# 8x8 window attention: rotated keys moved by a TensorE product and two masked ScalarE copies instead of eight DMA transfers

## The chip, the cores and the metric

The kernel runs on one core of a Trainium2 chip. The metric is device time in microseconds (us) of one execution of the whole program; lower is better. TensorE (PE in the profile; PEld are its weight loads), VectorE (DVE), ScalarE (ACT), GpSimd (POOL) and SyncE (SP, which here only issues transfers) run their own instruction streams and meet at semaphores.

## What is computed

An image of shape (4, 64, 64, 64) goes through five blocks: window attention over 8x8 windows, neighbourhood attention, a routed feed-forward block, retention and a binarised layer of experts. The change touches the first block alone:

```python
B, H, W, C = x.shape                 # 4, 64, 64, 64
hd = C // NH                         # 8 heads of 8
N = WH * WW                          # 64 tokens of an 8x8 window
xw = x.reshape(B, H // WH, WH, W // WW, WW, C).transpose(0, 1, 3, 2, 4, 5).reshape(-1, N, C)
qkv = xw @ qkv_w.T + qkv_b
qkv = qkv.reshape(-1, N, 3, NH, hd).transpose(2, 0, 3, 1, 4)
q, k, v = (qkv[0], qkv[1], qkv[2])
q = _rope2(q.reshape(-1, WH, WW, hd)).reshape(-1, NH, N, hd)
k = _rope2(k.reshape(-1, WH, WW, hd)).reshape(-1, NH, N, hd)
attn = jax.nn.softmax(q * hd ** (-0.5) @ jnp.swapaxes(k, -2, -1), axis=-1)
out = (attn @ v).transpose(0, 2, 1, 3).reshape(-1, N, C)
...
return out @ proj_w.T + proj_b
```

`_rope2` rotates pairs of channels of queries and keys by angles that depend on row and column in the window. The whole is `h = tok(x)`, then `h = h + block(layernorm(h))` four times.

## The kernel before

The five blocks run one after the other. The first, here "the 8x8 stage", takes 32 tiles of 512 tokens (8 windows). Its functions are named `tok_...`; each engine has a list of them per tile, and that written order is the order of execution: nothing reorders it. `pairs` unrolls two tiles (`par` 0 and 1) and loops over pairs, with the first and last pair written out. `T1[...]` are the stage's semaphores; `times(n)` is a count.

For tile i the work is, in the order of the data:

- SP `x_in` loads 512 tokens into `xin`. PE `tok_turn` transposes them into bank T (L503), ACT `tok_turned` copies them to `xT` (L869).
- PE `tok_qk` makes queries and keys in one product of 128x128 by 128x512 into bank T (L525) and the pairs' partners in a second of the same size into bank J1 (L526). Of 128 rows, each group of 32 has 8 for queries of a head, 8 for queries of another, then the keys of the same two.
- DVE `tok_rope` multiplies both by cosines and sines and adds them into `rot` (L1051, L1052, L1056).
- Queries and keys of a head stand in different partitions of `rot`, and a product contracts over equal partitions. So SP `k_in` moves the keys: for each of 4 groups of 32 rows and each of 2 heads one transfer of 8 rows by 512 (16 KB) from `rot` to `k_tok` (a view of `tile_a`), eight per tile (L322). The rows of `k_tok` that belong to no key of the head stay zero from a fill at the start.
- PE `tok_max` makes scores in bf16 to find the largest (L545), DVE `tok_max` reduces them (four reductions, L1077), PE `tok_top` transposes the maxima (L554), ACT copies them (L886), PE `tok_scores` makes scores minus maxima in 128 small products (L567 and L572), ACT takes four exponentials (L890).
- PE `tok_v` makes the values in bank T (L533), ACT `tok_v` copies them to `v_tok` in four copies (L879).
- PE `tok_values` makes the sums of the exponentials in bank OT, columns 0 to 255 (L583), and the weighted values in bank AV, columns 0 to 255 (L589). DVE `tok_normalize` takes the reciprocal (L1066) and multiplies into `aT1` (L1069).
- PE `tok_project` projects into bank OT, columns 256 to 511 (L600), DVE `tok_rows` adds the bias into `h` (L1061).

Tiles overlap. While PE works on the scores of tile i, DVE works ahead: its list for tile i is rows(i-1), max(i+1), normalize(i), rope(i+2). PE's is top(i), scores(i), project(i-1), v(i+1), values(i), turn(i+2), max(i+1), qk(i+2). ACT's is top(i), four exponentials (i), v(i+1), turned(i+2). SP's is x_in(i+3), k_in(i+2). The waits that matter for the change:

```python
def tok_max(i, par):                                   # PE
    pe.wait_ge(T1["k_in"], times((i + 1) * 128))
def tok_values(i, par):                                # PE
    pe.wait_ge(T1["exp_done"], times(i * 4 + 4))
    pe.wait_ge(T1["attn_out"], times(i))
    pe.wait_ge(T1["h_done"], times(i))                 # rows(i-1) has read bank OT
def k_in(i, par):                                      # SP
    sp.wait_ge(T1["rope"], times(i + 1))
```

Of the kernel before, what the change touches and what calls it, by code (L numbers as in the profile page):

```python
# [15 lines left out]
P = 128  # L16
# [28 lines left out]
def shape_tables():  # L45
# [14 lines left out]
    t["sin"] = (sin * scale).astype(np.float32)  # L60
    t["top_rows"] = np.broadcast_to((np.arange(P) % 32)[:, None, None] == np.arange(8)[None, :, None], (P, 8, C)).astype(np.float32)
# [36 lines left out]
def build(nc, a, out):  # L98
    ctx = ExitStack()
    with ctx:  # L100
# [21 lines left out]
        w_p1_rows, b_v1, bias1 = sb("w_p1_rows", [P, 2, C]), sb("b_v1", [P, P]), sb("bias1", [P, C])  # L122
        top_rows, ones_32 = sb("top_rows", [P, 8, C]), sb("ones_32", [P, 2, 32])
# [81 lines left out]
        T1 = named("tok", "x_in", "xT_ps", "xT_sb", "qk_ps", "rope_mul", "rope", "k_in", "v_ps", "v_sb", "max_ps", "max_done", "top_ps", "top_sb",  # L205
# [88 lines left out]
        def _(sp):  # L294
# [4 lines left out]
                     (w_p1[:, :], a["w_p1"]), (w_p1_rows[:, :, :], a["w_p1_rows"]), (b_v1[:, :], a["b_v1"]), (top_rows[:, :, :], a["top_rows"]),  # L299
# [17 lines left out]
            def k_in(i, par):  # L317
                sp.wait_ge(T1["rope"], times(i + 1))
                sp.wait_ge(T1["scores"], times((i - 1) * 2))
                for j in range(4):  # L320
                    for e in range(2):
                        sp.dma_start(k_tok[par][32 * j + HD * e:32 * j + HD * (e + 1), e, :],  # L322
                                     rot[32 * j + HD * (e + 2):32 * j + HD * (e + 3), par, :]).then_inc(T1["k_in"], 16)

            def tok(j, par):
                i = j * 2 + par
                if not isinstance(i, int) or i + 3 < NT:
                    x_in(i + 3)
                if not isinstance(i, int) or i + 2 < NT:
                    k_in(i + 2, par)  # L330

            sp.wait_ge(s_const, NCONST)
            x_in(0)
            x_in(1)
            k_in(0, 0)
            x_in(2)
            k_in(1, 1)
            pairs(sp, tok, 2)
# [94 lines left out]
        def _(gp):  # L433
# [3 lines left out]
                     (kpad[:, :, :], 0.0), (tile_a[:, :, :], 0.0), (tile_b[:, :, :], 0.0), (qk3[:, :], 0.0), (qd3[:, :], 0.0), (state[:, :, :], 0.0),  # L437
# [61 lines left out]
        def _(pe):  # L499
# [36 lines left out]
            def tok_max(i, par):  # L536
                pe.wait_ge(T1["k_in"], times((i + 1) * 128))
                for g in range(2):
                    pe.wait_ge(T1["exp_done"], times((i - 1) * 4 + 2 * g + 2))
                    settle(pe)  # L540
                    for p in range(4):
                        for ab in range(2):
                            for j in (2 * g, 2 * g + 1):
                                r = slice(32 * j, 32 * (j + 1))
                                mm = pe.matmul(s_tok[j][C * ab:C * (ab + 1), p * 128:(p + 1) * 128].rearrange("q (s k) -> q s k", s=2),  # L545
                                               top_half(rot[r, par, window(ab, p)]),
                                               k_tok[par][r, :, window(ab, p)].bitcast(BF16).rearrange("r s (k e) -> r s k e", e=2)[:, :, :, 1],
                                               start=True, stop=True)
                    mm.then_inc(T1["max_ps"], 1)
# [25 lines left out]
            def tok_values(i, par):  # L575
# [17 lines left out]
            def tok_project(i):  # L593
                pe.wait_ge(T1["attn_out"], times(i + 1))
                settle(pe)
                for y in range(4):
                    for y2 in range(2):
                        for ab in range(2):
                            at = 32 * (2 * y2 + ab)
                            mm = pe.matmul(bank["OT"][at:at + 32, 256 + y * C:256 + (y + 1) * C], aT1[:, 32 * (2 * y + y2):32 * (2 * y + y2 + 1)],  # L600
# [3 lines left out]
            def tok(j, par):  # L604
# [17 lines left out]
            tok_qk(0)  # L622
            tok_v(0)
# [238 lines left out]
        def _(act):  # L862
# [8 lines left out]

            def tok_v(i, par):
# [9 lines left out]
            def tok(j, par):  # L882
# [8 lines left out]
                if not last or i + 1 < NT:  # L891
                    tok_v(i + 1, 1 - par)
# [3 lines left out]
            tok_turned(0)  # L896
            tok_v(0, 0)
# [85 lines left out]
        def _(dve):  # L983
# [64 lines left out]
            def tok_rope(i, par):  # L1048
# [6 lines left out]
                dve.wait_ge(T1["k_in"], times((i - 1) * 128))  # L1055
                dve.tensor_tensor(rot[:, par, :], t_cos[:, :], t_sin[:, :], ALU.add).then_inc(T1["rope"], 1)  # L1056

            def tok_rows(i):
                dve.wait_ge(T1["proj"], times(i + 1))
                settle(dve)  # L1060
                dve.tensor_tensor(rows(i * 4, 4), bank["OT"][:, 256:512].rearrange("p (t c) -> p t c", t=4),  # L1061
                                  bias1[:, :].rearrange("p (a c) -> p a c", a=1).broadcast_to((P, 4, C)), ALU.add).then_inc(T1["h_done"], 1)

            def tok_normalize(i):
                dve.wait_ge(T1["av_done"], times(i + 1))
                dve.reciprocal(rec1[:, :], bank["OT"][:, 0:256]).then_inc(T1["rec_done"], 1)  # L1066
# [12 lines left out]
            def tok(j, par):  # L1079
# [151 lines left out]
NLOADS = 38  # L1231
NSTRIP = TOK // 256
NCONST = 28
# [60 lines left out]
```

## Time and profile before

| | us |
|---|---|
| median of 3 runs | 2614.84 |
| lowest, highest | 2593.13, 2616.89 |
| the profiled execution | 2611.62 |
| its span, first to last instruction | 2609.8 |
| PE busy in the span | 1993.9 |
| DVE busy | 1362.4 |
| ACT busy | 1059.0 |
| mean granted TensorE clock | 0.833 |

A busy PE is not PE at its peak, since matmuls overlap. The granted clock is the share of full speed that TensorE had: 1.00 is 2.4 GHz, 0.50 is 1.2 GHz, and there is no other level here. The 8x8 stage lies between about 40 us (first load done) and 551 us of the span. Idle time of an engine is put down to what came last by the profile; of several semaphores it may name the wrong one.

### The profile page before, as it was taken

What the parts mean: (1) busy time and instruction counts of PE and PEld (TensorE: products, weight loads), DVE (VectorE), ACT (ScalarE), POOL (GpSimd) and SP (SyncE); (2) the same over time, 40 slices, a digit from 0 to 9 for tenths busy, and PEclk for the clock granted to TensorE, in tenths of its full rate; (3) what the DMA queues carried; (4) which work ended last, traced back from release to release, by engine and by line L of the source; (5) the groups of instructions that cost most, each with busy time, mean ns of one, the idle gap of its engine ahead of it and who ended that gap; (6) DMA issues with size and microseconds to landing.
All of it is one profiled execution on the core that took longest, in us unless ns stands there. A gap on an engine that the chain in (4) does not pass through costs nothing.

```text
span 2609.8 us, 98500 instructions
## 1 busy us (share of the span) xinstructions
PE 1993.9 (76%) x37794; PEld 1494.9 (57%) x37794; DVE 1362.4 (52%) x3822; ACT 1059.0 (41%) x1826; POOL 451.5 (17%) x416
## 2 busy tenths in 40 slices
PE   2888888866588888888777877777777777777777
PEld 1655666544466666666555555555555555555555
DVE  2444444457444444444355556555566555665555
ACT  0222222223222222222245555555555555555555
POOL 2000000024222332332111111111111111111110
PEclk9777777778799999999878787788877888877888
DMA  2000000024433333333100000000000000000000
GB/s 90 20 19 16 16 17 16 16 62 103 95 91 96 92 93 96 92 92 95 44 9 9 11 9 10 9 9 10 10 10 9 9 9 11 10 9 9 9 11 6
DMA packets 221125, 94.80 MB, mean 36 GB/s; under 512 B 171090, under 2 KB 207762, under 8 KB 220818
## 3 DMA queue, kind: packets, MB, share of 16 engines
q1 hardware_dynamic: 221074, 94.08, 14.8%
q8 instruction: 37, 0.61, 0.1%
q14 instruction: 14, 0.11, 0.0%
HBM read 62.74 MB, written 18.42 MB: 31 GB/s over the span
## 4 chain that ended last, share of the span: by engine, by line
issue 34%; PE 21%; SPq 19%; DVE 12%; POOL 8%; ACT 3%; DVEq 1%; POOLq 0%; DMA 0%; ACTq 0%
SPq L391 10%; PE ps_D L761 4%; POOL rstd_ret L455 3%; ACT prob L945 3%; SPq L380 3%; POOL rstd_bin L455 3%; POOL rstd_ffn L455 2%; DVE prob L1168 2%; PE ps_OT L810 2%; PE ps_AV L771 2%; SPq L362 2%; PE ps_T L822 2%; PE ps_J L827 2%; PE ps_OT L811 1%; PE ps_J L817 1%
## 5 line engine op out<-in xcount | busy, mean ns | idle before, releaser
L945 ACT ACTIVATE prob<-ps_D 128x1024 bf16<-128x1024 f32 x512 | 516.5, 1024 | 254.0 <-PE ps_D L761 253.9
L1168 DVE TENSOR_TENSOR prob<-prob,xb 128x1024 bf16<-128x1024 bf16 x512 | 352.5, 689 | 129.2 <-ACT prob L945 123.3
L761 PE MATMUL ps_D<-g,w_parts 128*128 128x256 bf16 x2048 | 365.4, 309 | 4.3 <-ACT prob L945 0.2
L761 PEld LDWEIGHTS ps_D<-g,w_parts 128*128 128x128 bf16 x2048 | 213.5, 114 | 84.8 <-issue 31.7
L1123 DVE TENSOR_REDUCE m_sb<-ps_D 128x4 f32<-128x400 f32 x256 | 135.3, 570 | 209.7 <-PE ps_D L667 194.1
L933 ACT ACTIVATE prob<-ps_D 100x512 f32<-100x512 f32 x256 | 139.0, 595 | 218.3 <-PE ps_D L689 218.3
L771 PEld LDWEIGHTS ps_AV<-pair_sel,prob 128*128 128x128 bf16 x4096 | 185.0, 101 | 70.8 <-DVE prob L1168 47.1
L455 POOL TENSOR_TENSOR rstd_ffn<-veps_ffn,minus_half 128x2 f32<-128x2 f32 x64 | 59.3, 927 | 890.5 <-DVE veps_ffn L995 890.5
L771 PE MATMUL ps_AV<-pair_sel,prob 128*128 128x2 bf16 x4096 | 182.0, 165 | 40.2 <-DVE prob L1168 39.5
L470 POOL TENSOR_TENSOR tile_a<-q_st,q_mask 128x1024 f32<-128x1024 f32 x64 | 123.4, 1927 | 410.6 <-DMA q_st<-q_d 277.1
L503 PE MATMUL ps_T<-ident,xn_f 128*64 128x128 f32 x128 | 38.8, 407 | 196.8 <-DVE xn_f L1007 191.6
L1077 DVE TENSOR_REDUCE top<-ps_D 128x8 f32<-128x512 f32 x128 | 79.5, 683 | 192.7 <-PE ps_D L545 192.7
L689 PE MATMUL ps_D<-tile_a,key_patch 64*100 64x128 f32 x2048 | 177.4, 288 | 1.0 <-issue 1.0
L685 PE MATMUL ps_D<-mT,key_rows 64*100 64x128 bf16 x1024 | 129.9, 224 | 51.2 <-ACT mT L922 32.2
L689 PEld LDWEIGHTS ps_D<-tile_a,key_patch 64*100 64x100 f32 x2048 | 147.4, 166 | 1.4 <-issue 1.4
L503 PEld LDWEIGHTS ps_T<-ident,xn_f 128*64 128x64 f32 x128 | 11.7, 139 | 212.9 <-issue 212.9
L455 POOL TENSOR_TENSOR rstd_pre<-veps_pre,minus_half 128x4 f32<-128x4 f32 x32 | 32.7, 1022 | 544.1 <-DVE veps_pre L995 544.1
L572 PE MATMUL ps_D<-rot,tile_a 32*64 32x64 f32 x4096 | 124.2, 277 | 3.4 <-issue 3.4
L567 PE MATMUL ps_D<-top_T,top_rows 32*64 32x64 bf16 x2048 | 112.1, 221 | 16.6 <-ACT top_T L886 14.7
L572 PEld LDWEIGHTS ps_D<-rot,tile_a 32*64 32x64 f32 x4096 | 119.0, 175 | 5.8 <-issue 5.8
L685 PEld LDWEIGHTS ps_D<-mT,key_rows 64*100 64x100 bf16 x1024 | 79.9, 123 | 70.3 <-issue 70.3
L503 PE MATMUL ps_T<-ident,xn 128*64 128x128 f32 (+1 forms) x256 | 52.8, 314 | 82.5 <-DVE xn L1007 82.5
(159 smaller groups left out, 3948.9 us busy)
## 6 DMA issues: line engine op xcount, KB each, us to landing
tile_b<-v_d SPq DMA_DIRECT2D x640, 40.0 KB
key_st<-k_d SPq DMA_DIRECT2D x64, 175.0 KB, 3.0
key_st<-k_d SPq DMA_DIRECT2D x64, 167.0 KB, 3.0
w_exp<-experts SPq DMA_DIRECT2D x64, 129.0 KB, 2.2
k_d<-kpad SPq DMA_DIRECT2D x32, 140.0 KB, 2.3
xin<-in_x SPq DMA_DIRECT2D x32, 128.0 KB, 2.1
tile_a<-rot SPq DMA_DIRECT2D x256, 16.0 KB
q_d<-q_sb SPq DMA_DIRECT2D x32, 128.0 KB, 2.4
```

The lines of the kernel that those rows point to most:

```text
L391: sp.dma_start(v_patch[r * KS:(r + 1) * KS, par, :, :], bass.AP(src.tensor, src.offset, [[C, KS], [QP * C, 16], [1, C]])).then_inc(T2["v_i ...
L455: gp.tensor_tensor(rstd[:, :], veps[:, :], minus_half[:, 0:veps.shape[1]], ALU.pow).then_inc(q["rstd"], 1)
L470: gp.tensor_tensor(q_block[:, par, :].rearrange("c (p h q) -> c p h q", h=NH, q=NQ), q_st[:, :].rearrange("c (p a q) -> c p a q", a=1, q=N ...
L572: mm = pe.matmul(s_tok[j][m, at], k_tok[par][r, e, window(ab, p)], rot[r, par, window(ab, p)], start=False, stop=True)
L685: pe.matmul(s_loc[x][0:NKL, u * P:(u + 1) * P], top_half(key_rows[rows_of(x), par, at * NKL:(at + 1) * NKL]), mT[rows_of(x), par, :], star ...
L689: mm = pe.matmul(s_loc[x][0:NKL, u * P:(u + 1) * P], key_patch[rows_of(x), par, at * NKL:(at + 1) * NKL], q_block[rows_of(x), par, at * P: ...
L761: mm = pe.matmul(double[k % 2][:, u * 256:(u + 1) * 256], w_parts[:, (k * 4 + u) * P:(k * 4 + u + 1) * P], g3[:, half, :], start=True, sto ...
L771: mm = pe.matmul(bank["AV"][:, t * C + (k * 4 + u) * 2:t * C + (k * 4 + u) * 2 + 2], prod[:, k % 2, u * 256 + t * P:u * 256 + (t + 1) * P] ...
L933: act.activation(prob1[0:NKL, 2 * g + x, :], s_loc[x][0:NKL, :], ACT.Exp).then_inc(T2["exp_done"], 1)
L945: act.activation(sgn[:, k % 2, :], double[k % 2][:, :], ACT.Sign).then_inc(BN["sign"], 1)
L1123: dve.tensor_reduce(m_sb[:, C * x + HOT[x] + 4 * g:C * x + HOT[x] + 4 * g + 4], m_loc[x][:, 0:4 * NKL].rearrange("p (u n) -> p u n", u=4), ...
L1168: dve.tensor_tensor(prod[:, k % 2, :].rearrange("p (u n) -> p u n", u=4), sgn[:, k % 2, :].rearrange("p (u n) -> p u n", u=4), xb2[:, 1 - ...
```

## The change

Only the 8x8 stage changes, in four ways.

1. The eight transfers of `k_in` and the fill of `tile_a` go. A constant 128x128 matrix `key_shift` has a one where a key row of `rot` is to land in a query row. PE `tok_keys` multiplies `rot` by it into bank J1 (128x128 by 128x512, f32), and ACT `tok_keys` copies the bank twice into `k_tok`, each time scaled by one column of `head_row`, which is 1 in the rows of that head and 0 elsewhere. SP's list is left with `x_in` alone, in a plain loop. Two constants more are loaded.
2. DVE's list becomes rows(i-1), max(i+1), rope(i+2), normalize(i).
3. The sums of the exponentials go to bank AV, columns 256 to 511, beside the values; the projection goes to bank OT, columns 0 to 255. The wait for `h_done` moves from `tok_values` to `tok_project`.
4. PE's list becomes top(i), scores(i), keys(i+1), v(i+1), project(i-1), values(i), turn(i+2), max(i+1), qk(i+2); ACT's becomes top(i), four exponentials, keys(i+1), v(i+1), turned(i+2).

```diff
+    own = (np.arange(P)[:, None] == np.arange(P)[None, :] + 2 * HD) & (use < 2)[None, :]
+    t["key_shift"] = own.astype(np.float32)
+    t["head_row"] = (use[:, None] == np.arange(2)[None, :]).astype(np.float32)
...
-            def k_in(i, par):
-                sp.wait_ge(T1["rope"], times(i + 1))
-                sp.wait_ge(T1["scores"], times((i - 1) * 2))
-                for j in range(4):
-                    for e in range(2):
-                        sp.dma_start(k_tok[par][32 * j + HD * e:32 * j + HD * (e + 1), e, :],
-                                     rot[32 * j + HD * (e + 2):32 * j + HD * (e + 3), par, :]).then_inc(T1["k_in"], 16)
...
             x_in(0)
-            x_in(1)
-            k_in(0, 0)
-            x_in(2)
-            k_in(1, 1)
-            pairs(sp, tok, 2)
+            with sp.Fori(1, NT) as i:
+                x_in(i)
...
             def tok_qk(i):
                 pe.wait_ge(T1["xT_sb"], times(i + 1))
                 pe.wait_ge(T1["rope_mul"], times(i * 2))
+                pe.wait_ge(T1["k_sb"], times(i * 2))
...
+            def tok_keys(i, par):
+                pe.wait_ge(T1["rope"], times(i + 1))
+                settle(pe)
+                pe.matmul(bank["J1"][:, :], key_shift[:, :], rot[:, par, :], start=True, stop=True).then_inc(T1["k_ps"], 1)
...
             def tok_max(i, par):
-                pe.wait_ge(T1["k_in"], times((i + 1) * 128))
+                pe.wait_ge(T1["k_sb"], times((i + 1) * 2))
...
                 pe.wait_ge(T1["attn_out"], times(i))
-                pe.wait_ge(T1["h_done"], times(i))
...
-                        pe.matmul(bank["OT"][32 * j:32 * (j + 1), 0:256], ones_32[:, e, :],
+                        pe.matmul(bank["AV"][32 * j:32 * (j + 1), 256:512], ones_32[:, e, :],
...
             def tok_project(i):
                 pe.wait_ge(T1["attn_out"], times(i + 1))
+                pe.wait_ge(T1["h_done"], times(i))
...
                 tok_scores(i, par)
+                if not last or i + 1 < NT:
+                    tok_keys(i + 1, 1 - par)
+                    tok_v(i + 1)
                 if not last or i:
                     tok_project(i - 1)
-                if not last or i + 1 < NT:
-                    tok_v(i + 1)
                 tok_values(i, par)
...
+            def tok_keys(i, par):
+                act.wait_ge(T1["k_ps"], times(i + 1))
+                for e in range(2):
+                    act.activation(k_tok[par][:, e, :], bank["J1"][:, :], ACT.Copy, scale=head_row[:, e:e + 1]).then_inc(T1["k_sb"], 1)
...
-                tok_normalize(i)
                 if not last or i + 2 < NT:
                     tok_rope(i + 2, par)
+                tok_normalize(i)
```

PE's rows as they stand in the program, from the end of one tile's scores to the next tile's `tok_top` (`tile_a` is the keys, `tile_b` the values, `xT` the tokens). Before:

```order
L572 MATMUL ps_D<-rot,tile_a 64x64 x4
L600 MATMUL ps_OT<-w_p_rows,aT 32x64 x16
L533 MATMUL ps_T<-w_v,xT 64x64 x8
L583 MATMUL ps_OT<-prob,ones 32x256 x8
L589 MATMUL ps_AV<-prob,tile_b 32x64 x32
L503 MATMUL ps_T<-ident,xin 64x128 x4
L545 MATMUL ps_D<-tile_a,rot 64x128 x32
L525 MATMUL ps_T<-xT,w_qk 128x512
L526 MATMUL ps_J<-xT,w_qk_swap 128x512
```

The same place after the change:

```order
L564 MATMUL ps_D<-rot,tile_a 64x64 x4
L518 MATMUL ps_J<-rot,key_shift 128x512
L525 MATMUL ps_T<-w_v,xT 64x64 x8
L592 MATMUL ps_OT<-w_p_rows,aT 32x64 x16
L574 MATMUL ps_AV<-prob,ones 32x256 x8
L580 MATMUL ps_AV<-prob,tile_b 32x64 x32
L489 MATMUL ps_T<-ident,xin 64x128 x4
L537 MATMUL ps_D<-tile_a,rot 64x128 x32
L512 MATMUL ps_T<-xT,w_qk 128x512
L513 MATMUL ps_J<-xT,w_qk_swap 128x512
```

The key product stands between scores and values' weights, the projection has moved behind `tok_v`, and nothing else moved. DVE's rows of one tile, before:

```order
L1061 TENSOR_TENSOR h<-ps_OT,bias 128x256
L1077 TENSOR_REDUCE top<-ps_D 128x8 x4
L1066 RECIPROCAL rec<-ps_OT 128x256
L1069 TENSOR_TENSOR aT<-ps_AV,rec 128x4x8x8
L1051 TENSOR_TENSOR t_cos<-ps_T,cos 128x512
L1052 TENSOR_TENSOR t_sin<-ps_J,sin 128x512
L1056 TENSOR_TENSOR rot<-t_cos,t_sin 128x512
```

DVE's rows of one tile, after:

```order
L1061 TENSOR_TENSOR h<-ps_OT,bias 128x256
L1077 TENSOR_REDUCE top<-ps_D 128x8 x4
L1052 TENSOR_TENSOR t_cos<-ps_T,cos 128x512
L1053 TENSOR_TENSOR t_sin<-ps_J,sin 128x512
L1056 TENSOR_TENSOR rot<-t_cos,t_sin 128x512
L1066 RECIPROCAL rec<-ps_AV 128x256
L1069 TENSOR_TENSOR aT<-ps_AV,rec 128x4x8x8
```

The rotation stands ahead of the reciprocal and the product with it. ACT's rows of one tile after the change, with the two copies of the keys between exponentials and values:

```order
L885 ACTIVATE top_T<-ps_D 128x128
L889 ACTIVATE prob<-ps_D 128x512 x4
L869 ACTIVATE tile_a<-ps_J,head_row 128x512 x2
L878 ACTIVATE tile_b<-ps_T 64x4x4x8 x4
L863 ACTIVATE xT<-ps_T 64x512
```

Before, the same list without the row of L869.

## Rows read from the trace of the kernel before

**Rows 1.** The page: busy time, share of the span and instructions by engine.
```profile
PE 1993.9 (76%) x37794; PEld 1494.9 (57%) x37794; DVE 1362.4 (52%) x3822; ACT 1059.0 (41%) x1826; POOL 451.5 (17%) x416
```

**Rows 2.** Timeline of ACT, L886, once per tile: start, length, idle before.
```profile
60.64 0.28 ACT L886 ACTIVATE top_T<-ps_D 128x128 bf16<-128x128 f32 x1 [9.67 <-PE ps_D L554]
74.75 0.28 ACT L886 ACTIVATE top_T<-ps_D 128x128 bf16<-128x128 f32 x1 [2.81 <-PE ps_D L554]
88.92 0.28 ACT L886 ACTIVATE top_T<-ps_D 128x128 bf16<-128x128 f32 x1 [3.09 <-PE ps_D L554]
...
535.81 0.28 ACT L886 ACTIVATE top_T<-ps_D 128x128 bf16<-128x128 f32 x1 [9.00 <-PE ps_D L554]
```

**Rows 3.** Waits of PE from 137.51 to 506.19 us: total us, times, longest.
```profile
PE ps_D L545 <- DMA tile_a<-rot: 38.4, 12, 3.2
```

**Rows 4.** Windows: length, busy us of PE, PEld, DVE, ACT, POOL, granted clock, DMA.
```profile
137.51:506.19 368.68, 305.94 (x8664) 222.40 (x8664) 165.20 (x241) 93.83 (x240) 0.00 (x0) 0.72 0.09 17
...
302.66:316.32 13.66, 9.67 (x364) 6.98 (x362) 6.88 (x10) 4.50 (x11) 0.00 (x0) 1.00 0.09 19
316.32:333.39 17.07, 15.83 (x360) 11.56 (x361) 6.88 (x10) 3.32 (x9) 0.00 (x0) 0.50 0.08 16
```

**Rows 5.** Windows of an early stretch, the same columns.
```profile
77.38:84.20 6.82, 6.32 (x156) 4.76 (x150) 1.32 (x3) 2.53 (x8) 0.00 (x0) 0.50 0.10 19
```

**Rows 6.** Timeline of PE: start, length, work, idle before.
```profile
302.90 0.55 PE L545 MATMUL ps_D<-tile_a,rot 32*64 32x128 bf16 x32
303.84 1.10 PE L525 MATMUL ps_T<-xT,w_qk 128*128 128x512 f32 x2 [0.39 <-ACT xT L869]
304.78 1.02 PE L526 MATMUL ps_J<-xT,w_qk_swap 128*128 128x512 f32 x2
...
309.56 0.65 PE L600 MATMUL ps_OT<-w_p_rows,aT 128*32 128x64 f32 x32
310.15 0.68 PE L533 MATMUL ps_T<-w_v,xT 64*64 64x64 f32 x16
311.33 1.07 PE L583 MATMUL ps_OT<-prob,ones 128*32 128x256 f32 x16 [0.50 <-ACT tile_b L879]
...
313.30 0.60 PE L503 MATMUL ps_T<-ident,xin 128*64 128x128 f32 x4
317.10 0.81 PE L545 MATMUL ps_D<-tile_a,rot 32*64 32x128 bf16 x32 [3.20 <-DMA tile_a<-rot]
317.84 2.08 PE L525 MATMUL ps_T<-xT,w_qk 128*128 128x512 f32 x2
319.71 1.91 PE L526 MATMUL ps_J<-xT,w_qk_swap 128*128 128x512 f32 x2
...
333.62 0.56 PE L545 MATMUL ps_D<-tile_a,rot 32*64 32x128 bf16 x32
```

**Rows 7.** Timeline of DVE in the same tile as the first rows of group 6.
```profile
305.78 1.75 DVE L1066 RECIPROCAL rec<-ps_OT 128x256 f32<-128x256 f32 x1
...
309.40 0.69 DVE L1056 TENSOR_TENSOR rot<-t_cos,t_sin 128x512 f32<-128x512 f32 x1 [0.22 <-DVE t_sin L1052]
310.65 0.42 DVE L1061 TENSOR_TENSOR h<-ps_OT,bias 128x256 f32 x1 [0.55 <-PE ps_OT L600]
```

**Rows 8.** Timeline of ACT in the same tile.
```profile
309.67 1.09 ACT L890 ACTIVATE prob<-ps_D 128x512 f32<-128x512 f32 x2 [0.17 <-PE ps_D L572]
310.88 0.89 ACT L879 ACTIVATE tile_b<-ps_T 64x128 f32<-64x128 f32 x4
```

**Rows 9.** Timeline of SP: issue of two constants, and of one tile's eight key transfers.
```profile
11.79 1.05 SPq L310 DMA_DIRECT2D key_rows<-in_key_rows  x2
...
310.21 5.32 SPq L322 DMA_DIRECT2D tile_a<-rot  x8
```

**Rows 10.** Timeline of PE, the first tile's `tok_max`.
```profile
56.01 0.81 PE L545 MATMUL ps_D<-tile_a,rot 32*64 32x128 bf16 x32 [5.67 <-DMA tile_a<-rot]
```

**Rows 11.** Timeline of DVE, the last step of the 8x8 stage.
```profile
550.79 0.42 DVE L1061 TENSOR_TENSOR h<-ps_OT,bias 128x256 f32<-128x256 f32 x1 [0.98 <-PE ps_OT L600]
```

More of the change, by code:

```diff
@@ L122, in build @@
         w_p1_rows, b_v1, bias1 = sb("w_p1_rows", [P, 2, C]), sb("b_v1", [P, P]), sb("bias1", [P, C])
+        key_shift, head_row = sb("key_shift", [P, P]), sb("head_row", [P, 2])
         top_rows, ones_32 = sb("top_rows", [P, 8, C]), sb("ones_32", [P, 2, 32])
@@ L203, in settle @@
             eng.sem_inc(s_settled, 1)
-        T1 = named("tok", "x_in", "xT_ps", "xT_sb", "qk_ps", "rope_mul", "rope", "k_in", "v_ps", "v_sb", "max_ps", "max_done", "top_ps", "top_sb",
+        T1 = named("tok", "x_in", "xT_ps", "xT_sb", "qk_ps", "rope_mul", "rope", "k_ps", "k_sb", "v_ps", "v_sb", "max_ps", "max_done", "top_ps", "top_sb",
                    "scores", "exp_done", "av_done", "rec_done", "attn_out", "proj", "h_done")
@@ L298, in _ @@
                      (decay_k[:, :], a["decay_k"]), (w_qk[:, :], a["w_qk"]), (w_qk_swap[:, :], a["w_qk_swap"]), (w_v1[:, :], a["w_v1"]),
-                     (w_p1[:, :], a["w_p1"]), (w_p1_rows[:, :, :], a["w_p1_rows"]), (b_v1[:, :], a["b_v1"]), (top_rows[:, :, :], a["top_rows"]),
+                     (w_p1[:, :], a["w_p1"]), (w_p1_rows[:, :, :], a["w_p1_rows"]), (b_v1[:, :], a["b_v1"]), (top_rows[:, :, :], a["top_rows"]), (key_shift[:, :], a["key_shift"]), (head_row[:, :], a["head_row"]),
                      (w_kq2[:, :], a["w_kq2"]), (w_v2[:, :], a["w_v2"]), (w_p2[:, :, :], a["w_p2"]), (bias2[:, :], a["b_p2"].broadcast_to((P, C))),
@@ L436, in _ @@
                      (ones_row[:, :], 0.0), (ones_row[0:1, :], 1.0), (minus_half[:, :], -0.5), (zeros[:, :], 0.0),
-                     (kpad[:, :, :], 0.0), (tile_a[:, :, :], 0.0), (tile_b[:, :, :], 0.0), (qk3[:, :], 0.0), (qd3[:, :], 0.0), (state[:, :, :], 0.0),
+                     (kpad[:, :, :], 0.0), (tile_b[:, :, :], 0.0), (qk3[:, :], 0.0), (qd3[:, :], 0.0), (state[:, :, :], 0.0),
                      (g3[:, :, :], 0.0), (w_parts[:, :], 0.0), (experts[:, :, NEXP:NEXP + 1, :], 0.0),
@@ L599, in tok_project @@
                             at = 32 * (2 * y2 + ab)
-                            mm = pe.matmul(bank["OT"][at:at + 32, 256 + y * C:256 + (y + 1) * C], aT1[:, 32 * (2 * y + y2):32 * (2 * y + y2 + 1)],
+                            mm = pe.matmul(bank["OT"][at:at + 32, y * C:(y + 1) * C], aT1[:, 32 * (2 * y + y2):32 * (2 * y + y2 + 1)],
                                            w_p1_rows[:, ab, :], start=True, stop=True)
@@ L622, in _ @@
             tok_qk(0)
+            tok_keys(0, 0)
             tok_v(0)
@@ L891, in tok @@
                 if not last or i + 1 < NT:
+                    tok_keys(i + 1, 1 - par)
                     tok_v(i + 1, 1 - par)
@@ L896, in _ @@
             tok_turned(0)
+            tok_keys(0, 0)
             tok_v(0, 0)
@@ L1054, in tok_rope @@
                 dve.wait_ge(T1["scores"], times((i - 1) * 2))
-                dve.wait_ge(T1["k_in"], times((i - 1) * 128))
                 dve.tensor_tensor(rot[:, par, :], t_cos[:, :], t_sin[:, :], ALU.add).then_inc(T1["rope"], 1)
@@ L1060, in tok_rows @@
                 settle(dve)
-                dve.tensor_tensor(rows(i * 4, 4), bank["OT"][:, 256:512].rearrange("p (t c) -> p t c", t=4),
+                dve.tensor_tensor(rows(i * 4, 4), bank["OT"][:, 0:256].rearrange("p (t c) -> p t c", t=4),
                                   bias1[:, :].rearrange("p (a c) -> p a c", a=1).broadcast_to((P, 4, C)), ALU.add).then_inc(T1["h_done"], 1)
@@ L1065, in tok_normalize @@
                 dve.wait_ge(T1["av_done"], times(i + 1))
-                dve.reciprocal(rec1[:, :], bank["OT"][:, 0:256]).then_inc(T1["rec_done"], 1)
+                dve.reciprocal(rec1[:, :], bank["AV"][:, 256:512]).then_inc(T1["rec_done"], 1)
                 dve.wait_ge(T1["rec_done"], times(i + 1))
@@ L1228, in _ @@
             staggered(dve, strips)
-NLOADS = 38
+NLOADS = 40
 NSTRIP = TOK // 256
-NCONST = 28
+NCONST = 27
 def _with_bias(w, b):
```

6 lines of the change are left out of this document (removed).

## The prediction

> **What bounds the kernel now.** I read the page first. PE is the busiest engine by far [rows 1], but a share over five blocks says nothing about one of them, so the next view is the one row that ACT writes per tile of the 8x8 stage, L886 [rows 2]. From 60.64 to 535.81 us it comes 32 times, so 31 tiles take 475.2 us, 15.33 us each. The change touches these 475 us, the fill before them and the tail behind them, and nothing of the other 2,060 us.
>
> Inside, PE is busy 305.9 of 368.7 us, at a mean granted clock of 0.72 [rows 4]. Its largest wait is for the eight key transfers: 38.4 us in 12 of 24 tiles, 3.2 us each [rows 3]. Every second tile waits, and the windows show why the others don't. The stage alternates between 13.66 us at clock 1.00 and 17.07 us at 0.50, together two tiles [rows 4]. In the fast stretch PE reaches the key wait at 313.90 and the transfers land at 317.10; the clock is at half from 316.32, just behind this wait [rows 4, 6]. At half speed PE takes so much longer that the next keys are there in time: 333.62 has no wait in its row [rows 6]. So the stage is bound by PE, and the transfers cost twice: once as 3.2 us of waiting, once by what follows, 17 us at half clock.
>
> The chain behind the wait: DVE's `rot` ends at 310.09 [rows 7], SP issues eight transfers in 5.32 us from 310.21 [rows 9], and 317.10 is 7.0 us behind `rot`.
>
> **The change part by part.** First the price of a tile in which PE waits for no keys.
>
> At full clock, from 302.90 (`tok_max`) to the end of `tok_turn` at 313.30 + 0.60 = 313.90 is 11.00 us [rows 6]. Of this 0.50 us is the wait ahead of the sums at 311.33. The row names ACT, which is not plausible for a copy that starts at 310.88; DVE's `h` ends at 310.65 + 0.42 = 311.07 and `tok_values` waits for it because sums and projection share bank OT [rows 6 to 8]. The sums move to bank AV, so I take the 0.50 off. The new product is 128x128 by 128x512 in f32, as L525 is, which takes 304.78 - 303.84 = 0.94 us. New tile at full clock: 11.00 - 0.50 + 0.94 = 11.44 us.
>
> At half clock, from 317.10 to 333.62 is 16.52 us without a wait for keys or `h` [rows 6]. The product is 319.71 - 317.84 = 1.87 us. New tile at half clock: 18.39 us.
>
> Do the new steps wait for anybody? I put them into the fast tile of group 6, where slack is least.
> - `tok_keys(i+1)` needs `rot` of the next tile. Before, the rotation stood behind the reciprocal (1.75 us from 305.78) and its product (about 0.42, as the bias add of that size takes), and ended at 310.09, 0.5 us after the scores gave way at 309.56 [rows 6, 7]. Now it goes ahead of these 2.2 us and ends near 308. It is hidden by the scores, with 1.5 us to spare. Without the third part of the change PE would wait 0.7 us here.
> - What is late instead is `aT1`, now at about 310.3, for the projection. That one has moved behind key product and `tok_v`: 309.56 + 0.94 + 0.68 = 311.2. Slack 0.9 us.
> - ACT finishes the exponentials at 309.67 + 1.09 = 310.76, then two copies of 128x512. No row shows this form. The nearest is the exponential of the same size, two in 1.09 us [rows 8], and I take that: 310.76 to 311.95 with the start behind it. The values' four copies (0.89 us) end at 312.85. PE wants the keys at `tok_max`, about 314.3, the bank T free at `tok_turn`, about 313.7. Slack 0.8 us. From below the copies could cost half of it, from above twice (2.2 us); then `tok_turn` would wait 0.3 us, 9 us over the stage.
> - SP loses all but one transfer per tile; nobody is queued behind it. `xin` is still asked for when `tok_turn` has read it and has a whole tile to land.
>
> The Trainium skill has something against this way of copying: ScalarE: Activation LUTs, section "What ACT_TABLE_LOAD costs", adds about 93 ns for a scale that is a column in memory. No row here shows such a copy. By it the two take 1.3 us, the slack shrinks by 0.2 us to 0.6, and the sum stays.
>
> Now the clock, which decides more than all of this. If a tile spends the share s of its time at half clock, PE does 1/11.44 of a tile per us at full and 1/18.39 at half, so it lasts 11.44 / (1 - 0.378 s). Before, s was 17.07 of 30.73, 0.56. The trigger in the steady part, the wait for keys, is gone. It isn't the only trigger, however: at 77.38 the clock fell for 6.8 us although PE had waited for no transfer, while it did the small products of the scores, which leave most of the array idle [rows 5]. That tile took 88.92 - 74.75 = 14.17 us [rows 2]. In the steady fast stretches, one of which is in group 4, the scores ran through without a fall. I take the middle between a fall in no tile (s = 0) and one in each (6.8 of 14.2, s = 0.48), a fall in every second tile: s = 0.25, 12.63 us per tile.
>
> The skill's page TensorE: Matmul & The Clock Gate, section "Why this matters for your kernels", asks for no idle gaps between bursts of matmuls and promises the full clock for it. The fall at 316.32 behind the wait agrees with it, the one at 77.38 does not. By the page alone s would be 0 and the time 2486; by the rows it is 2524.
>
> The sum, against the profiled execution of 2611.6:
> - 31 tiles x (15.33 - 12.63) = 83.7 us less.
> - Start: two more loads, as issued two constants take 1.05 us [rows 9]. The first `tok_max` stands at 56.01 behind a wait of 5.67 us for keys [rows 10], so its `rot` was there 7.0 us earlier, at 49.0. The new path from there is key product (1.87), two copies (1.2), the values' copies behind them (0.9) and `tok_turn` (0.6 at full clock, 1.0 taken), 54.0. Together 2.0 - 1.05, 1.0 us less.
> - Tail: from 535.81 to 551.21 [rows 2, 11] are 15.4 us, the same work at about the same mix; at 12.63/15.33 of it, 2.7 us less.
> - Together 87.4: 2524.2 us. The profiled execution is 3 us under the median of the three runs, which themselves spread by 24 us.
>
> **The rivals.**
> - *The clock never falls* (s = 0). For it: scores at full clock ran through in the steady stretches. 31 x 3.89 = 120.6, tail 3.9, start 1.0: 2486 us.
> - *It falls as often as before* (s = 0.48 to 0.56), because the cause is the mixture of small products and not the wait. Tiles of 13.98 to 14.48 us save 42 to 26 us, with tail and start 2567 to 2584.
> - *It falls in each tile and the extra product is paid in full*: the early tile of 14.17 us had no key wait already. With 0.94 to 1.87 us on top it is 15.1 to 16.0, against 15.33. Then the time is 2604 to 2632, no change. Against it: that tile stood in the first pass through the code and contains stalls of issue of its own.
> - *Slower*: the stage locks at half clock. The price is 31 x 3.06 = 95 us, 2709 with the tail; it decides from s = 0.67, where the new tile reaches 15.33. For it: PE was busy 15.83 of 17.07 us and the clock still stayed at half [rows 4], and the change takes idle time away, not small products. Against it: each such stretch of the trace ended at the sums and values, and the new order puts key product, `tok_v`, projection, sums and values in one unbroken piece: at full clock 0.94 + (313.30 - 309.56 - 0.50) = 4.2 us, at half 1.87 + 3.24 x 16.52 / 10.50 = 7.0 us [rows 6].
> - *ScalarE becomes late*: 9 us more by the bound above, 2533, inside the first case.
>
> **How the numbers follow.** Between s = 0.1 and 0.45 (2500 to 2562): 0.50. No falls to speak of: 0.17. As often as before: 0.14. In each tile at full price: 0.12. Slower: 0.07. The time is that of the first, 2524. The range 2484 to 2586 takes in the first three. About 1% is what a measurement of this kernel can tell from no change, 26 us; the first three lie beyond it, so faster 0.81, same 0.12, slower 0.07.
>
> **What the profile after would show.** L886 once in 11.4 to 14 us, 12.6 in the mean. No wait for `tile_a` ahead of the bf16 scores, and none ahead of the sums. Windows of half clock that begin inside the scores and fill a quarter of the stage. The key product at 0.94 and 1.87 us, behind the scores without a wait; two ACT copies in 1.1 to 1.3 us that end before `tok_turn`. I would be wrong if the granted clock of the stage stayed at 0.72 or below, if PE waited for ACT at `tok_turn` or for `aT1` at the projection, or if a tile at full clock took over 12 us.

## The result, and the profile after

| | before | after |
|---|---|---|
| median, us | 2613.26 (4 runs) | 2510.65 (4 runs) |
| lowest, highest | 2593.13, 2616.89 | 2504.36, 2517.65 |
| the profiled execution | 2611.62 | 2515.59 |
| its span | 2609.8 | 2513.8 |
| mean granted clock | 0.833 | 0.871 |

The ratio is 0.962, 95% interval 0.957 to 0.967. The change is faster by 3.8%; 2524 was forecast. One run of the kernel before, measured beside runs 9 to 12, took 8405.6 us and is in none of the ratios.

The page's first part for the kernel after, as in [rows 1]:

```profile
PE 1930.8 (77%) x37858; PEld 1442.6 (57%) x37858; DVE 1363.8 (54%) x3822; ACT 1093.4 (43%) x1890; POOL 464.0 (18%) x415
```

64 matmul records more (two per product), ACT 34 us more, DVE the same. ACT's row once per tile, as in [rows 2]:

```profile
60.02 0.28 ACT L885 ACTIVATE top_T<-ps_D 128x128 bf16<-128x128 f32 x1 [3.87 <-PE ps_D L546]
...
105.61 0.28 ACT L885 ACTIVATE top_T<-ps_D 128x128 bf16<-128x128 f32 x1 [2.75 <-PE ps_D L546]
122.48 0.28 ACT L885 ACTIVATE top_T<-ps_D 128x128 bf16<-128x128 f32 x1 [2.74 <-PE ps_D L546]
133.76 0.28 ACT L885 ACTIVATE top_T<-ps_D 128x128 bf16<-128x128 f32 x1 [2.75 <-PE ps_D L546]
...
442.43 0.28 ACT L885 ACTIVATE top_T<-ps_D 128x128 bf16<-128x128 f32 x1 [4.49 <-PE ps_D L546]
```

31 tiles take 382.4 us, 12.34 us each, where it was 15.33. Twenty of them last 11.28 to 11.31 us, as from 122.48 to 133.76; these run at clock 1.00 throughout and are called full tiles below. They look like this on PE (timeline of the kernel after, to be laid beside [rows 6]):

```profile
215.59 0.55 PE L537 MATMUL ps_D<-tile_a,rot 32*64 32x128 bf16 x32
216.44 1.10 PE L512 MATMUL ps_T<-xT,w_qk 128*128 128x512 f32 x2 [0.29 <-ACT xT L863]
217.37 1.02 PE L513 MATMUL ps_J<-xT,w_qk_swap 128*128 128x512 f32 x2
218.70 0.30 PE L546 MATMUL ps_D<-ident,top 128*128 128x128 f32 x1 [0.31 <-DVE top L1077]
...
222.25 1.12 PE L518 MATMUL ps_J<-rot,key_shift 128*128 128x512 f32 x2
223.31 0.68 PE L525 MATMUL ps_T<-w_v,xT 64*64 64x64 f32 x16
223.92 0.65 PE L592 MATMUL ps_OT<-w_p_rows,aT 128*32 128x64 f32 x32
224.39 1.07 PE L574 MATMUL ps_AV<-prob,ones 128*32 128x256 f32 x16
...
226.88 0.55 PE L537 MATMUL ps_D<-tile_a,rot 32*64 32x128 bf16 x32
...
233.53 2.00 PE L518 MATMUL ps_J<-rot,key_shift 128*128 128x512 f32 x2
```

No row waits for keys, for `h` or for the rotation. What PE mainly waits for still is in its waits from 123 to 442 us, as in [rows 3]:

```profile
PE ps_D L559 <- ACT top_T L885: 12.4, 27, 0.5
PE ps_D L546 <- DVE top L1077: 9.5, 27, 1.5
PE ps_T L512 <- ACT xT L863: 7.6, 26, 0.3
```

The clock, as in [rows 4]: the first four tiles, the other 27, and one fall of the clock, with the stretch of its tile ahead of it.

```profile
60.02:122.48 62.46, 50.89 (x1420) 33.82 (x1420) 25.55 (x38) 20.22 (x49) 0.00 (x0) 0.81 0.05 12
122.48:442.43 319.95, 289.43 (x9793) 200.95 (x9793) 186.84 (x271) 135.32 (x324) 0.00 (x0) 0.95 0.06 14
226.88:233.60 6.72, 5.66 (x231) 4.02 (x230) 6.09 (x8) 1.96 (x4) 0.00 (x0) 1.00 0.09 20
233.60:237.02 3.42, 3.42 (x39) 1.80 (x42) 0.42 (x1) 2.54 (x6) 0.00 (x0) 0.51 0.00 0
```

From 0.73 the clock rises to 0.95 for 27 tiles. It still falls: at 233.60, just behind the scores, although PE had been idle for nothing longer than 0.46 us in this tile. This fall lasts 3.4 us, and its tile 12.82 us instead of 11.28. Of the six falls between the fifth and the thirtieth tile two are of this kind; the other four last 6.8 us each, in tiles of 14.4 us.

### The profile page after: what moved, and what is told of

Same layout as the page of the kernel before. It is cut to its first block, busy times and chain, and to the rows that moved or that the text cites. A ratio compares the mean times of both kernels' runs of the same rounds, so it can differ in the third digit from the quotient of the medians.

```text
span 2513.8 us, 98479 instructions
## 1 busy us (share of the span) xinstructions
PE 1930.8 (77%) x37858; PEld 1442.6 (57%) x37858; DVE 1363.8 (54%) x3822; ACT 1093.4 (43%) x1890; POOL 464.0 (18%) x415
## 3 DMA queue, kind: packets, MB, share of 16 engines
q1 hardware_dynamic: 217266, 89.94, 14.4%
## 4 chain that ended last, share of the span: by engine, by line
issue 32%; PE 27%; SPq 14%; DVE 13%; POOL 8%; ACT 4%; DMA 1%; DVEq 1%; POOLq 0%; ACTq 0%
SPq L377 6%; PE ps_D L755 4%; ACT prob L946 3%; POOL rstd_ffn L441 3%; POOL rstd_ret L441 2%; POOL rstd_bin L441 2%; PE ps_AV L765 2%; DVE prob L1168 2%; PE ps_T L489 2%; SPq L348 2%; PE ps_OT L804 2%; SPq L366 2%; PE ps_T L816 2%; PE ps_J L821 2%; PE ps_J L811 1%
## 5 line engine op out<-in xcount | busy, mean ns | idle before, releaser
L441 POOL TENSOR_TENSOR rstd_ffn<-veps_ffn,minus_half 128x2 f32<-128x2 f32 x64 | 73.7, 1151 | 880.4 <-DVE veps_ffn L996 880.4
L1192 DVE TENSOR_SCALAR g<-ps_J 24x256 bf16<-24x256 f32 x64 | 26.3, 412 | 159.8 <-PE ps_J L811 159.8
L950 ACT ACTIVATE xnT<-ps_T 64x256 f32<-64x256 f32 x64 | 24.2, 378 | 191.3 <-PE ps_T L489 191.3
L923 ACT ACTIVATE mT<-ps_T 128x128 bf16<-128x128 f32 x64 | 17.8, 278 | 204.0 <-PE ps_T L668 204.0
```

The costliest lines, as they stand in the source:

```text
L441: gp.tensor_tensor(rstd[:, :], veps[:, :], minus_half[:, 0:veps.shape[1]], ALU.pow).then_inc(q["rstd"], 1)
```

## The experiments

All times are medians, with the ratio to the kernel before measured beside them. "Tile" is the distance of ACT's rows in the profiled execution; a "fall" is a stretch at 0.50 that begins in the 31 tiles.

**1. The transfers put back, the rest kept.**

```diff
-            with sp.Fori(1, NT) as i:
-                x_in(i)
+            x_in(1)
+            k_in(0, 0)
+            x_in(2)
+            k_in(1, 1)
+            pairs(sp, tok, 2)
...
-                    tok_keys(i + 1, 1 - par)
```

> The changed kernel with the eight key transfers put back in place of the product and the two copies; VectorE's new order, the sums beside the values and PE's new order are kept. Theory (a loop through the transfers): before, tok_max at 302.90 and the keys' arrival at 317.10 are 14.2 us apart; the rotation now stands 2.2 us earlier, so the loop is 12.0 us. PE's own work at full clock is 11.28 - 0.94 = 10.3 us, so PE waits 1.7 us per tile. If such a wait does not pull the clock down, tiles take 12.0 to 13 us and the time is 2510 to 2540. Rival (any wait for keys pulls the clock down): tiles of 14.5 to 15.3 us, 2585 to 2613.

Measured: 2547.3 us, ratio 0.974 (0.969 to 0.980). PE's largest wait from 124 to 466 us, and two rows of its timeline that are one tile apart:

```profile
PE ps_D L549 <- DMA tile_a<-rot: 29.5, 20, 1.9
```
```profile
167.25 0.59 PE L549 MATMUL ps_D<-tile_a,rot 32*64 32x128 bf16 x32 [1.67 <-DMA tile_a<-rot]
...
179.35 0.59 PE L549 MATMUL ps_D<-tile_a,rot 32*64 32x128 bf16 x32 [1.54 <-DMA tile_a<-rot]
```

The loop is there: 12.10 us per tile at full clock, 12.0 expected, with 1.67 us of waiting in it. The time is 7 us above the range expected, and the clock falls 19 times and not 10; 29% of the stage is at half. Seven of the 19 begin 1.0 to 1.7 us behind the end of a wait for keys, where the kernel after has none, so such a wait does cost clock, as the rival said, but not in every tile. Still, with the transfers in place the kernel gains 63 us from the other three parts of the change together. That it is the rotation ahead of the normalisation follows from the loop, 2.1 us shorter as computed; this run does not take the parts apart.

**2. The product and the copies alone in the kernel before.**

```diff
                 if not last or i:
                     tok_project(i - 1)
                 if not last or i + 1 < NT:
+                    tok_keys(i + 1, 1 - par)
                     tok_v(i + 1)
```

> The kernel before with the key product and the two masked copies alone: old VectorE order, sums in bank OT behind the wait for h, projection ahead of the product. Theory: at full clock 11.0 us, plus 0.94 for the product, plus 0 to 0.2 of waiting for the rotation, that is 12.0 us, and falls of the clock as in the changed kernel (0.7 to 1.0 us per tile): 12.8 us, 2535. Rival (the order and the bank carry the gain, or the product only makes PE longer): tiles of 14 us and more, 2575 or above.

Measured: 2527.3 us, ratio 0.9665 (0.961 to 0.972). Full tiles last 11.40 us, 0.12 more than after the whole change, and there are 14 falls. So the first part alone brings 83 of 100 us. Runs 1 and 2 gain 63 and 83 us, together far more than the whole: they shorten the same loop at two places. 12.0 us were expected for a full tile, and 12.8 in the mean, which is what it has: the full tiles are shorter and the falls more than expected. PE does the projection while the rotation ends, and the wait for `h` is covered by the product: among the waits of run 2 from 123 to 456 us neither has a row.

**3. The wait for keys filled with dense products, in the kernel before.** The three products write a bank that nobody reads any more.

```diff
             def tok_max(i, par):
+                pe.wait_ge(T1["rope_mul"], times((i + 1) * 2))
+                settle(pe)
+                for _ in range(3):
+                    pe.matmul(bank["J1"][:, :], w_qk[:, :], cos[:, :], start=True, stop=True)
                 pe.wait_ge(T1["k_in"], times((i + 1) * 128))
```

> The kernel before with three products of 128x128 by 128x512 (0.94 us each at full clock) put ahead of tok_max, where PE waits 3.2 us for the keys; their result is not used. Theory (the idle wait is what pulls the clock down): the clock no longer falls behind it, nearly all tiles run at full clock, and the loop through the transfers of 14.2 us sets the pace: 31 x 1.1 us less, 2575 to 2585. Rival (the clock falls through the small products of the scores, whatever PE does in the wait): half the time at half clock with 5.6 us of added work in such a tile, 2613 to 2660.

Measured: 2613.5 us, ratio 1.001 (0.998 to 1.004), the same. Its stage in the window view, and the rows around one filler:

```profile
59.35:531.54 472.19, 409.16 (x11337) 276.89 (x11337) 211.07 (x308) 120.51 (x309) 0.00 (x0) 0.90 0.09 18
```
```profile
166.70 2.74 PE L540 MATMUL ps_J<-cos,w_qk 128*128 128x512 f32 x6
170.05 0.59 PE L549 MATMUL ps_D<-tile_a,rot 32*64 32x128 bf16 x32 [0.60 <-DMA tile_a<-rot]
```

The clock does what the first theory says: 0.90 instead of 0.73, and the falls at the wait are gone. The time does not. Two tiles of three last 14.2 us, the loop through the transfers, as computed; in each third one the clock falls in the scores and it lasts 16.0 us; the first four tiles take 69.5 us where they took 61.3. The time lies at the lower edge of the rival's range, but not for the rival's reason, since 20% of the stage is at half clock and not half of it; the first theory has the loop right and the remaining falls wrong. What follows is more than either said: before the change, a clock that never fell could not have brought the tiles under 14.2 us. The half clock of the kernel before cost 15.33 - 14.2 = 1.1 us per tile, and the loop through VectorE, SP and the transfers cost the rest of the distance to 11.3 us.

**4, 10. The gap behind the transposed maxima filled, in the kernel after.** The product writes a bank that the scores overwrite. Run 10 repeats run 4 with the kernel after (run 9) beside it.

```diff
                 pe.transpose(s_tok[3][:, 0:P], top1[:, :, :].rearrange("q j n -> q (j n)"), ident[:, :]).then_inc(T1["top_ps"], 1)
+                pe.matmul(s_tok[0][:, 0:256], w_qk[:, :], cos[:, 0:256], start=True, stop=True)
```

> The changed kernel with one product of 128x128 by 128x256 (0.47 us at full clock) between tok_top and the scores, where PE is idle for 0.46 us in each tile; its result is overwritten. Theory (the ten falls of the clock in the stage start where small products follow the idle gaps of tok_top): falls vanish outside the first tiles, six of about 2.2 us each, 13 us less: 2495 to 2500. Rival (the falls have to do with the small products alone): as many falls, and the filler costs 0 to 0.5 us per tile: 2510 to 2520.

> The changed kernel with the 128x128 by 128x256 product in the idle 0.46 us behind tok_top, on the same chip as the changed kernel. Theory (the clock falls where the small products of the scores follow an idle gap; filled, it stays): 31 x 0.6 us less than the changed kernel, 2495 to 2503, at most three falls in the stage, all in the first tiles. Rival (the 8 us seen before are scatter between jobs): the same time as the changed kernel within 4 us.

Measured: 2502.6 us, ratio 0.958 (0.953 to 0.964), and the second time 2503.9 us, 0.9585 (0.955 to 0.962); both lie above the ranges expected, by 2.6 and 0.9 us. The kernel after, run once more beside the second:

> The changed kernel itself once more, as the reference for the three beside it. Both theories: 2505 to 2515, ratio 0.962 to the kernel before.

Measured: 2510.5 us, ratio 0.962 (0.959 to 0.966). The stage of run 9 and of run 10 in the window view, and ACT's rows of run 4:

```profile
58.48:438.88 380.40, 338.06 (x11213) 235.18 (x11213) 212.32 (x308) 155.25 (x372) 0.00 (x0) 0.93 0.06 14
```
```profile
58.95:424.67 365.72, 336.78 (x11276) 233.82 (x11275) 212.41 (x308) 155.14 (x372) 0.00 (x0) 0.98 0.06 15
```
```profile
140.17 0.28 ACT L886 ACTIVATE top_T<-ps_D 128x128 bf16<-128x128 f32 x1 [2.75 <-PE ps_D L546]
151.45 0.28 ACT L886 ACTIVATE top_T<-ps_D 128x128 bf16<-128x128 f32 x1 [2.75 <-PE ps_D L546]
162.73 0.28 ACT L886 ACTIVATE top_T<-ps_D 128x128 bf16<-128x128 f32 x1 [2.75 <-PE ps_D L546]
```

In both profiles no tile from the fifth to the thirtieth is longer than 11.32 us; run 4 has two falls, run 10 four in the first four tiles and one in the last. The falls of the kernel after from the fifth to the thirtieth tile (6 in its first profile, 4 in run 9) are gone with a product of no use in 0.46 us of idle time. The stage is 15 to 19 us shorter than in either profile of the kernel after, but the profiled executions of runs 4 and 10 (2496.7 and 2493.6 us) are also 6 and 10 us below their own medians. Between the medians there are 7 us in runs 9 and 10, and 8 us between run 4 and the first measurement of the kernel after; the intervals of the ratios still touch, so the times alone don't tell the two kernels apart with certainty. The mean granted clock of each whole execution does: 0.871 to 0.876 in all ten of the kernel after, 0.877 to 0.881 in all ten with the product.

**11, 12. What of the filler counts.** One uses a corner of the array, the other lasts half as long.

```diff
+                pe.matmul(s_tok[0][0:64, 0:256], w_qk[0:32, 0:64], cos[0:32, 0:256], start=True, stop=True)
```
```diff
+                pe.matmul(s_tok[0][:, 0:128], w_qk[:, :], cos[:, 0:128], start=True, stop=True)
```

> As before, but the filler uses a corner of the array only: 32 rows by 64 columns of weights, 256 columns streamed, so PE is as little idle as with the full product. Theory A (what counts is how much of the array works): falls as in the changed kernel, 2505 to 2515. Theory B (what counts is that PE is not idle): no falls, 2495 to 2503.

> As before, but the filler is half as long: 128x128 by 128x128, 0.23 us at full clock, which leaves half of the gap idle. Theory (work of the full array in this stretch keeps the clock up): fewer falls than the changed kernel's ten, down to the two or three of the first tiles if half is enough: 2497 to 2508. Rival (the gap has to be closed): falls as in the changed kernel, 2505 to 2515.

Measured: 2503.0 us, ratio 0.959 (0.954 to 0.963), and 2504.3 us, 0.959 (0.954 to 0.963). The times tell nothing apart. The traces do in part. ACT's rows of run 11, with a tile of 14.42 us:

```profile
139.86 0.28 ACT L886 ACTIVATE top_T<-ps_D 128x128 bf16<-128x128 f32 x1 [2.75 <-PE ps_D L546]
151.14 0.28 ACT L886 ACTIVATE top_T<-ps_D 128x128 bf16<-128x128 f32 x1 [2.74 <-PE ps_D L546]
165.56 0.28 ACT L886 ACTIVATE top_T<-ps_D 128x128 bf16<-128x128 f32 x1 [2.74 <-PE ps_D L546]
```

With the corner product three such tiles remain between the fifth and the thirtieth, 116 us apart like three of the four in run 9; with the short full one there is none, and one of 17.25 us behind them, the last. By these two profiles the full array would count and not the idle time, although the longer of the two products was the corner's. The clocks of the other executions say something else: 0.878, 0.879 and 0.881 with the corner product, as high as with the full one of that length, and only the profiled one is low, at 0.875. With the short full product, which leaves half of the gap idle, they are 0.876, 0.876, 0.877 and 0.879, between the two kernels. So most of the executions, and the medians, side with the second theory of run 11, that what counts is that PE is not idle. But these clocks are means over all five blocks: in the profiled executions of these kernels 576 to 592 us are at half clock outside the 31 tiles and 17 to 59 us within, so a difference of one or two falls can come from elsewhere. How much the size of the product counts stays open.

**5. VectorE normalises first again, in the kernel after.**

```diff
+                tok_normalize(i)
                 if not last or i + 2 < NT:
                     tok_rope(i + 2, par)
-                tok_normalize(i)
```

> The changed kernel with VectorE's old order: reciprocal and product ahead of the rotation. Theory: in a tile at full clock the rotation ends at 220.56 and the scores at 222.25; 2.2 us later it would end at 222.7, and the key product starts 0.65 us later, 20 us over 31 tiles: 2525 to 2535. Rival (the order is hidden by the scores either way): 2505 to 2515.

Measured: 2545.6 us, ratio 0.976 (0.972 to 0.980). PE's wait from 124 to 472 us:

```profile
PE ps_J L518 <- DVE rot L1056: 10.7, 21, 0.5
```

A full tile is 11.83 us, 0.55 more (0.65 expected). That is 17 us. The other 18 us go with the clock: 14 falls instead of 10 and 8 in the two profiles of the kernel after, 24% of the stage at half instead of 13 to 15%. The mechanism was right, and the price nearly double, 11 us above the range expected.

**6. The sums back in bank OT, in the kernel after.**

```diff
                 pe.wait_ge(T1["attn_out"], times(i))
+                pe.wait_ge(T1["h_done"], times(i))
...
-                        pe.matmul(bank["AV"][32 * j:32 * (j + 1), 256:512], ones_32[:, e, :],
+                        pe.matmul(bank["OT"][32 * j:32 * (j + 1), 0:256], ones_32[:, e, :],
```

> The changed kernel with the sums back in bank OT and the wait for h back ahead of them. Theory: the projection is now directly ahead of the sums, so they wait for it, for VectorE's 0.42 us of bias add and for two semaphores, 1.2 us per tile at full clock: 37 us, 2540 to 2550. Rival (the wait is the 0.5 us it was before): 15 us, 2525.

Measured: 2553.9 us with runs from 2537.9 to 2584.8, ratio 0.984 (0.976 to 0.991). PE's wait from 127 to 464 us:

```profile
PE ps_OT L575 <- ACT tile_b L878: 28.1, 27, 1.1
```

1.1 us per tile, 1.2 expected. The name ACT is again the wrong one: the bank and the wait for `h` are all that was changed. In the profiled execution, which is the fastest of the four, the clock stays up: three falls, all in the first tiles, tiles of 12.44 and 12.58 us afterwards, mean clock 0.878. There the wait costs its own length and no clock. The others are not like it: 2548.7 us go with a mean clock of 0.874, 2559.0 with 0.867 and 2584.8 with 0.859. Their traces were not taken, so whether it fell in this stage is not known, and that the wait costs no clock is shown for one execution alone. Without the highest, which lies apart, the median is 2548.7 us, inside the range expected.

**7. The product twice.**

```diff
+                pe.matmul(bank["J1"][:, :], key_shift[:, :], rot[:, par, :], start=True, stop=True)
                 pe.matmul(bank["J1"][:, :], key_shift[:, :], rot[:, par, :], start=True, stop=True).then_inc(T1["k_ps"], 1)
```

> The changed kernel with the key product made twice. Theory: it lies on PE's path, 0.93 us at full clock and 1.9 at half, 29 us and more, less some falls of the clock that the dense product may avoid: 2530 to 2545. Rival (it hides in waits, or brings the clock up so much that it costs nothing): 2500 to 2515.

Measured: 2550.0 us, ratio 0.978 (0.974 to 0.982). A full tile is 12.17 us, 0.89 more (0.93 expected); the stage takes 419.0 us, 37 to 39 more than in the two profiles of the kernel after. 28 us of it are the product at full clock, the rest clock and the first four tiles (64.9 us instead of 62.5). The time is 5 us above the range expected. The product is paid in full, and a dense product here buys no clock: 13 falls, and a mean clock of 0.871 to 0.874 in the four executions.

**8. Four ScalarE copies more**, written to places unused in this stage.

```diff
+                for dst in (q_sb[:, 0, :], q_sb[:, 1, :], key_patch[:, 0, 0:512], key_patch[:, 1, 0:512]):
+                    act.activation(dst, bank["J1"][:, :], ACT.Copy, scale=head_row[:, 0:1])
```

> The changed kernel with four more ScalarE copies of 128x512 ahead of the two of the keys, written elsewhere. Theory: in a full tile the values' copies end at 225.46 and PE wants the bank at 226.35, a slack of 0.9 us; four copies are 2.4 us, so tok_turn waits 1.5 us per tile, 47 us: 2550 to 2565. Rival (the wait pulls the clock down as the key wait did): tiles of 14 us and more, 2590 or above. Second rival (ScalarE has more room than read): 2510 to 2530.

Measured: 2566.9 us, ratio 0.9855 (0.981 to 0.990). PE's wait from 123 to 488 us:

```profile
PE ps_T L489 <- ACT tile_b L880: 32.1, 21, 1.5
```

A full tile is 12.82 us, 1.54 more (1.5 expected), and the time is 2 us above the range. So ScalarE's slack in the kernel after is the 0.9 us read from the trace. The 1.5 us of idle PE do not lock the clock at half, but they do bring falls: there are 21, on 22% of the stage, and 13 of them begin 1.4 to 2.0 us behind the end of this wait, where the kernel after has none.

## Why the prediction was right, point by point

**The tile at full clock.** 11.44 us were forecast, 11.28 measured. The product is 223.31 - 222.25 = 1.06 us start to start, 0.94 forecast. The rest of the tile is 0.28 us shorter than the sum from [rows 6]. The wait ahead of the sums is gone as said (224.39 follows 223.92 without one). From the start of `tok_v` over the projection to the sums it is 1.08 us; before, the same two took 1.27, the wait taken off; and `tok_qk` follows `tok_max` by 0.85 us instead of 0.94, behind a shorter wait for `xT`. Run 7 gives the product's price by doubling it, 0.89 us.

**The slacks.** The rotation ends ahead of the scores, at 220.56 against 222.25, 1.7 us where 1.5 were forecast: run 5 takes 2.2 us away and PE waits 0.5. (The prediction calls this order the third part of the change; it is the second.) `aT1` makes nobody wait. The two copies, in ACT's timeline of the same tile:

```profile
223.41 1.27 ACT L869 ACTIVATE tile_a<-ps_J,head_row 128x512 f32<-128x512 f32 x2
224.57 0.89 ACT L878 ACTIVATE tile_b<-ps_T 64x128 f32<-64x128 f32 x4
```

They take 1.27 us where the exponentials in [rows 8] took 1.09, 0.09 us more for each, and the values' copies end at 225.46, 0.9 us ahead of `tok_turn` (0.8 forecast). The Trainium skill (ScalarE: Activation LUTs, "What ACT_TABLE_LOAD costs") adds about 93 ns for a scale that is a column in memory, and this trace agrees. It changed nothing, since run 8 had to add 2.4 us of copies to make PE wait 1.5.

**The clock.** s = 0.25 was forecast, 0.15 measured (58.6 of 382.4 us). With 11.28 us and that share the formula gives 11.28 / (1 - 0.378 x 0.153) = 11.97 us, and 12.34 was measured. This is the term that was mis-sized twice, in opposite directions. Falls are rarer than "every second tile": 10 in 31 tiles, 6 of them behind the first four and ahead of the last. And the first four tiles, 62.5 us, are no faster than before (61.3). Part of the reason is stalls of PE that end by nothing the profile shows, in its waits from 60 to 123 us:

```profile
PE ps_D L564 <- issue: 4.5, 2, 2.2
...
PE ps_D L559 <- issue: 1.2, 1, 1.2
PE ps_J L518 <- issue: 1.0, 1, 1.0
```

With one of 0.5 us more they make 7.2 us. But the kernel before had such stalls too, 5.6 us in its waits from 60 to 122 us, of which these are the largest:

```profile
PE ps_D L572 <- issue: 3.0, 2, 1.8
PE ps_D L567 <- issue: 1.9, 1, 1.9
```

And among those waits of the kernel before there is none for keys: in the first four tiles the change had no such wait to take away, and it added a product to each. I had applied one mean to all 31 tiles. Behind them 27 tiles take 319.95 us, 11.85 each, and save 93.9 us; with their own share at half clock, 0.11, the formula gives 11.76, so the formula holds where the tiles are steady. That 12.63 us came near the measured 12.34 is partly luck: the full tile and s were taken too high, and the first four tiles, left out, made up for some of it. With 11.85 us in all 31 tiles the forecast would have been about 2499 us.

**The reason given for the old time was half wrong.** I wrote that the stage was bound by PE and that the clock decided more than all else, and that the clock fell just behind the key wait. By [rows 4, 6] it fell at 316.32, inside this wait and 0.8 us ahead of its end. Runs 1 and 3 show another reading of the same rows: `tok_max` at 302.90 and the keys' arrival at 317.10 [rows 6] are a loop of 14.2 us that was already at full clock (`tok_max`, VectorE's maxima, normalisation and rotation, the transfers, the next `tok_max`). Half clock added 1.1 us to it. The forecast still came out, because both of its ends, the old 15.33 us and the new 11.44 us, were measured or summed without that claim.

**Which rival.** "The clock never falls" was nearer than it looked: run 10 comes closest to that case, with 5% of the stage at half. It took 2503.9 us and not 2486. In its profiled execution, 2493.6 us, the first four tiles take 60.0 us, 15 more than four full ones; why the median is 10 us above this execution stays open. Falls "in each tile at full price" and "slower" did not come; run 7, with a tile that has 0.89 us more, doesn't come near 15.3 either. The Trainium skill (TensorE: Matmul & The Clock Gate, "Why this matters for your kernels") asks for bursts of matmuls without long idle gaps between them. Run 3 agrees for the falls at the key wait, and the fall at 233.60 differs from it, with no gap over 0.46 us ahead of it in its tile.

**The sum.** Against the profiled execution: tiles 92.8 us less (83.7 forecast), the start 60.64 - 60.02 = 0.6 (1.0), the tail 0.9 (2.7), everything behind the stage 1.8 (nothing): 96.0 us where 87.4 were forecast. The tail's end is DVE's last row of the stage, as in [rows 11]:

```profile
456.56 0.42 DVE L1061 TENSOR_TENSOR h<-ps_OT,bias 128x256 f32<-128x256 f32 x1 [1.32 <-PE ps_OT L592]
```

## What to carry to other kernels

Where two tiles alternate between a wait and a slow clock, follow the loop from one use of a buffer to the next before blaming the clock: its length is the floor, and anything taken out of it anywhere (a transfer, or merely the order in which VectorE does two things) comes off every tile, until the busiest engine's own sequence is longer than the loop (here PE's 11.3 us, of which 1.1 are short waits). A move between partitions that costs eight small transfers can be a product and two masked copies. Here the copies fitted into ScalarE's slack and were free, and the product was paid in full on PE, 0.9 us per tile, against a loop that was 2.9 us longer than the tile is now. And price a change in a pipelined stage tile by tile where the first tiles differ: here the first four had no wait for keys, and the change saved nothing in them. Last, one profiled execution can be the exception of its kernel: in runs 6 and 11 the mean clocks of the others are unlike its own.

## What the runs showed of the hardware that was not expected

The clock fell while PE was idle for no more than 0.3 to 0.5 us at a time, in or just behind the small products of the scores (32 rows by 64 columns). One product of the full array of 0.47 us per tile in an idle place stopped that behind the first tiles (runs 4 and 10), and the mean granted clock of its ten executions, 0.877 to 0.881, lies above all ten of the kernel after, 0.871 to 0.876. A product of the same number of columns on a corner of the array left three falls in the profiled execution of run 11 (0.875), and its three others have 0.878 to 0.881.

Waits of PE of 1.1 to 1.9 us did not bring a fall each time, and not at every place. Ahead of the sums, 1.1 us in 27 tiles brought none in the profiled execution of run 6, though the clocks of the other three are lower. Ahead of `tok_turn`, 1.5 us in 21 tiles brought 13 falls, which begin 1.4 to 2.0 us behind its end (run 8). Ahead of `tok_max`, up to 1.9 us in 20 tiles brought 7 (run 1). What decides between them no run here shows.
